# A four-network graph kernel: the nodes' update and the next products as one stage between two edge loops

## What is computed

```python
h = h @ W_in + b_in
def layer(hc, p):
    w1, b1, w2, b2, m1, c1, m2, c2 = p
    m = jnp.concatenate([hc[row], hc[col]], axis=1)
    m = jax.nn.silu(m @ w1 + b1)
    m = jax.nn.silu(m @ w2 + b2)
    agg = jax.ops.segment_sum(m, row, num_segments=N)
    z = jax.nn.silu(jnp.concatenate([hc, agg], axis=1) @ m1 + c1)
    return (hc + (z @ m2 + c2), None)
h, _ = jax.lax.scan(layer, h, (eW1, eb1, eW2, eb2, nW1, nb1, nW2, nb2))
return h @ W_out + b_out
```

## Time and profile before

| | |
|---|---|
| Median of three runs | 12523.31 us (12512.99 to 12532.43) |
| The profiled execution, its own time | 12525.73 us |
| Its span in the trace | 12523.9 us |
| Busy in the span: PE, DVE, ACT, POOL | 9274.0, 5811.6, 1419.6, 8101.0 us |
| Mean granted clock of PE | 0.764 of full |

### The profile page before, as it was taken

The page is one execution under the profiler, slowest core; times in us unless marked ns, Lnnn a source line. Parts: engine busy times, 40 slices in busy tenths (PEclk is TensorE's granted clock), DMA queues, the critical chain, the costliest instruction groups (busy, mean ns, idle before and its releaser), DMA issues. The chain is left out here.

```text
span 12523.9 us, 184074 instructions
## 1 busy us (share of the span) xinstructions
PE 9274.0 (74%) x46241; PEld 7382.7 (59%) x46242; DVE 5811.6 (46%) x14093; ACT 1419.6 (11%) x2535; POOL 8101.0 (65%) x8276
## 2 busy tenths in 40 slices
PE   3777888777677767776777899999993558785333
PEld 1665444566566656665666677777763547674333
DVE  9773000344344434443444455555557754443333
ACT  0002333111111111111111000000000001110000
POOL 3777777777477747774776577776760007775776
PEclk6557889677777777777777899999995658886555
DMA  1333443222222222222222687777772212221111
GB/s 56 102 109 124 142 136 129 65 52 52 40 65 52 52 54 52 52 52 42 52 52 41 169 205 204 205 204 204 203 190 60 87 44 64 64 63 30 26 26 26
DMA packets 818891, 1141.33 MB, mean 91 GB/s; under 512 B 245286, under 2 KB 442294, under 8 KB 817332
## 3 DMA queue, kind: packets, MB, share of 16 engines
q1 hardware_dynamic: 367186, 610.56, 17.7%
q0 software_dynamic: 277888, 340.47, 13.0%
q10 hardware_dynamic: 173666, 188.57, 4.6%
HBM read 939.74 MB, written 199.09 MB: 91 GB/s over the span
## 5 line engine op out<-in xcount | busy, mean ns | idle before, releaser
L1086 POOL DMA_INDIRECT gx_l<-xr,gi_l x4160 | 4007.4, 963 | 2579.8 <-DVE gi_l L1170 1314.5
L1575 PE MATMUL psum<-cw,xa 128*128 128x256 f32 (+1 forms) x8320 | 2116.0, 397 | 0.0
L1575 PEld LDWEIGHTS psum<-cw,xa 128*128 128x128 f32 (+1 forms) x8320 | 1442.6, 189 | 611.7 <-issue 482.4
L1192 DVE TENSOR_TENSOR aggT_l<-aggT_l,psum 64x128 f32 x4160 | 1158.6, 279 | 865.3 <-DVE aggT_l L1192 727.7
L1243 PE MATMUL psum<-ptab,oht 128*128 x6656 | 1176.6, 351 | 378.1 <-issue 204.5
L1243 PEld LDWEIGHTS psum<-ptab,oht 128*128 128x128 f32 x6656 | 1116.0, 262 | 477.4 <-issue 476.0
L1204 DVE TENSOR_TENSOR pre_s_l<-psum,gx_l 128x512 f32<-128x512 f32 x520 | 359.6, 691 | 1988.2 <-DMA gx_l<-xr,gi_l 1929.6
L1563 POOL DMA_INDIRECT wkv<-wtab,ei x832 | 908.5, 1092 | 453.4 <-issue 364.1
L706 POOL DMA_INDIRECT slots_s<-rec_s,row_s x806 | 812.2, 1008 | 399.9 <-issue 395.7
L1556 POOL DMA_INDIRECT gx<-xr,gi x832 | 788.4, 948 | 373.4 <-issue 252.9
L2133 POOL DMA_INDIRECT gx_l<-xr,gi_l x832 | 797.1, 958 | 332.8 <-issue 237.1
(11 more groups left out here) (341 smaller groups left out, 11934.1 us busy)
## 6 DMA issues: line engine op xcount, KB each, us to landing
shb<-shT SPq DMA_DIRECT2D x1872, 128.0 KB
kr<-keyrow_s SPq DMA_DIRECT2D x416, 256.0 KB
gx_l<-xr,gi_l POOLq DMA_INDIRECT x4992
wtab<-eo ACTq DMA_DIRECT2D x152, 512.0 KB, 4.0
vtab<-kv ACTq DMA_DIRECT2D x208, 256.0 KB, 2.4
v_in<-vtab SPq DMA_DIRECT2D x104, 512.0 KB, 3.3
hT<-noderow SPq DMA_DIRECT2D x101, 512.0 KB
kr<-keyrow_d SPq DMA_DIRECT2D x208, 128.0 KB
```

Of the source, the lines that this page charges most:

```text
L1086: pool.indirect_dma_start(gx[j][:, c_, :], None, xr, bass.IndirectOffsetOnAxis(ap=gi[j][:, c_:c_ + 1], axis=0)).then_inc(rows_in[j].sem, 16)
L1192: ins = dve.tensor_tensor(a, a, sums(j, h), ALU.add)
L1575: ins = pe.matmul(bank[2 + p][:, t % 2 * OKV:(t % 2 + 1) * OKV], xa[j][0:n_, c, t * P:(t + 1) * P], cw[0:n_, c, :], start=c == 0, stop=c = ...
```

## The change

The ten loads get three semaphores: product weights, edge weights, node weights. Layer 0's products are formed once ahead of the loop. Then each layer is an edge loop and one node stage. In that stage PE writes the first products alternately to banks 0, 1 and 2, 3, the second ones to banks 4 and 5, and the next layer's products (in the last layer the output's) to banks 6 and 7, straight from hT; its written order is first(0), first(1), second(0), first(2), second(1), products(0), first(3), and so on. z1T and qst have a second buffer each. The bias is split at the stage's start, aggT cleared at its end. Between layers one join is left, ahead of the edge loop. The chunks' column copies, turning and eviction stand at the start of the edge loop, where PE then waits until all is evicted; SP stores the features and loads the node weights, the next chunks and the next product weights inside the loop, behind its third key load. Behind the last layer the output stage is gone, and the layer norm stands ahead of the keys' copies.

```diff
+        qst_b = chunks.enter_context(nc.sbuf_tensor("qst_b", [P, CH, D], F32))
...
-        def edge_messages(o, local, feature=None):
+        def edge_messages(o, local, feature=None, opening={}):
...
                         sp.dma_start(kr[j][:], keyrow[o][bass.ds(i * (W * P), W * P)].partition_broadcast(P)).then_inc(keys_in[j].sem, 16)
+                        if k.fixed and k.t == 2 and "sp" in opening:
+                            opening["sp"]()
...
             join()
+            if "chunk" in opening:
+                opening["chunk"]()
...
-            join()
+            if feature:
+                join()
...
+        qsts = [qst, qst_b]
+        z1s = [z1T, hcur]
...
+        def product_weights_sp(l):
+            w1_in.at(sp.dma_start(w1[:], L0_eW1[l:l + 1, :, :].rearrange("a (k p) f -> p (a k) f", p=P)), 16)
+            w1_in.at(sp.dma_start(b1[:], L0_eb1[l:l + 1, :].rearrange("a f -> (a f)").partition_broadcast(P)), 16)
+            w1_in.at(sp.dma_start(b2r[:], L0_eb2[l:l + 1, :].rearrange("a f -> (a f)").partition_broadcast(3)), 16)
...
+        def edge_weights_sp(l):
+            for k in range(2):
+                w2_in.at(sp.dma_start(w2[k * D:(k + 1) * D, k * D:(k + 1) * D], L0_eW2[l:l + 1, :, :].rearrange("a p f -> p (a f)")), 16)
...
+        def node_weights_sp(l):
+            m_in.at(sp.dma_start(m1a[:], L0_nW1[l:l + 1, 0:HID, :].rearrange("a p f -> p (a f)")), 16)
...
+        def first_products():
+            product_weights_sp(0)
+            edge_weights_sp(0)
+            node_weights_sp(0)
+            dve.wait_ge(w1_in.sem, w1_in.n)
+            split_bias(b2r[:], b2[:], b2w)
+            pe.wait_ge(w1_in.sem, w1_in.n)
+            meet()
+            node_products(hcur, hT, w1)
+            scatters_end()
+            dve.memset(aggT[:], 0.0)
+            sp.wait_ge(w2_in.sem, w2_in.n)
+            sp.nop(nofuse=True)
...
         def layer(l):
-            wi = loaded
-            wi.at(sp.dma_start(w1[:], L0_eW1[l:l + 1, :, :].rearrange("a (k p) f -> p (a k) f", p=P)), 16)
...
-            wi.at(sp.dma_start(c2[:], L0_nb2[l:l + 1, :].rearrange("a (p f) -> p (a f)", f=1)), 16)
-            if l > 0:
...
+            last = l + 1 == LAYERS
+
+            def while_edges_sp():
...
+                if l:
+                    features_out_sp(l)
+                    node_weights_sp(l)
+                if not last:
+                    chunk_sp(l + 1)
+                    product_weights_sp(l + 1)
+
+            def chunk_first():
+                chunk_dve(l)
                 chunk_pe(l)
                 chunk_act(l)
-            dve.wait_ge(wi.sem, wi.n)
-            split_bias(b2r[:], b2[:], b2w)
-            meet()
-            node_products(hcur, hT, w1)
-            if l == 0:
-                scatters_end()
-            else:
-                chunk_dve(l)
-                features_out_sp(l)
-            step(dve.memset(aggT[:], 0.0))
-            if l + 1 < LAYERS:
-                chunk_sp(l + 1)
-            edge_messages("s", gather_p)
-            z_silu, z2_done, h_set = sig("z_silu"), sig("z2"), sig("h_set")
-
...
+            edge_messages("s", gather_p, opening={"sp": while_edges_sp, "chunk": chunk_first} if l else {"sp": while_edges_sp})
+            node_stage(l, last)
+
+        def node_stage(l, last):
+
+            added = sig("added")
+            z_silu, z2_done, h_set, formed, p_kept, summed_up = (sig(x) for x in ("z_silu", "z2", "h_set", "formed", "p_kept", "x_added"))
+            out_ps = bank[6][:, 0:CH * D].rearrange("p (b f) -> p b f", f=D)
+            next_ps = PS[:, 6 * 512:6 * 512 + CHN].rearrange("p (b k f) -> p b k f", b=CH, k=2)
+
+            def stage_pe():
+                pe.wait_ge(added.sem, added.n)
+                pe.wait_ge(m_in.sem, m_in.n)
+                pe.wait_ge(w1_in.sem, w1_in.n)
+                pe.nop(nofuse=True)
...
+                def first_of_two(i):
+                    if i >= 2:
...
-                        ins = pe.matmul(bank[k][:, 0:HALF], m1b[:], aggT[:, s_], start=False, stop=True)
+                        to = bank[2 * (i % 2) + k][:, 0:HALF]
+                        pe.matmul(to, m1a[:], hT[:, s_], start=True, stop=False)
+                        ins = pe.matmul(to, m1b[:], aggT[:, s_], start=False, stop=True)
...
+                def second_of_two(i):
                     pe.wait_ge(z_silu.sem, z_silu.n + i + 1)
                     if i:
                         pe.wait_ge(h_set.sem, h_set.n + i)
...
+                        ins = pe.matmul(bank[4 + k][:, 0:HALF], m2[:], z1s[i % 2][:, k * HALF:(k + 1) * HALF], start=True, stop=True)
                     ins.then_inc(z2_done.sem, 1)
...
-            def update_act():
+                def products(i):
+                    pe.wait_ge(h_set.sem, h_set.n + i + 1)
+                    if i and last:
+                        pe.wait_ge(summed_up.sem, summed_up.n + i)
+                    elif i:
+                        pe.wait_ge(p_kept.sem, p_kept.n + i)
+                        pe.wait_ge(evicted.sem, evicted.n + i)
...
+                    for b in range(CH):
+                        h_ = hT[:, i * CHN + b * P:i * CHN + (b + 1) * P]
...
+                            ins = pe.matmul(PS[:, 6 * 512 + b * P:6 * 512 + (b + 1) * P], h_, w1[:].rearrange("p k f -> p (k f)"), start=True, stop=True)
+                    ins.then_inc(formed.sem, 1)
+
+                first_of_two(0)
+                first_of_two(1)
                 for i in range(NCH):
+                    second_of_two(i)
+                    if i:
+                        products(i - 1)
+                    if i + 2 < NCH:
+                        first_of_two(i + 2)
+                products(NCH - 1)
+
...
+                def silu(i):
                     act.wait_ge(product.sem, product.n + i + 1)
-                    if i:
...
-                    act.activation(z1T[:].rearrange("p (k n) -> p k n", k=2), halves(0), ACT.Silu, bias=c1[:, 0:1]).then_inc(z_silu.sem, 1)
...
+                    if i >= 2:
+                        act.wait_ge(z2_done.sem, z2_done.n + i - 1)
...
+                    act.activation(z1s[i % 2][:].rearrange("p (k n) -> p k n", k=2), of, ACT.Silu, bias=c1[:, 0:1]).then_inc(z_silu.sem, 1)
...
+                def evict(i):
+                    act.wait_ge(p_kept.sem, p_kept.n + i + 1)
+                    if i >= 2:
+                        act.wait_ge(kept_in[i % 2].sem, kept_in[i % 2].n + 16 * (i // 2))
+                    act.copy(qsts[i % 2][:], next_ps[:, :, 1, :]).then_inc(evicted.sem, 1)
+
+                silu(0)
+                silu(1)
                 for i in range(NCH):
+                    if i and not last:
+                        evict(i - 1)
+                    if i + 2 < NCH:
+                        silu(i + 2)
+                if not last:
+                    evict(NCH - 1)
...
+                if not last:
+                    split_bias(b2r[:], b2[:], b2w)
...
+                    dve.scalar_tensor_tensor(s_, halves(4), c2[:, 0:1], s_, ALU.add, ALU.add).then_inc(h_set.sem, 1)
...
+                def keep(i):
+                    dve.wait_ge(formed.sem, formed.n + i + 1)
+                    dve.tensor_tensor(ptab[:, i * CH * D:(i + 1) * CH * D].rearrange("p (b f) -> p b f", f=D), next_ps[:, :, 0, :],
...
+                def add(i):
+                    dve.wait_ge(formed.sem, formed.n + i + 1)
+                    s_ = xn[:, i * CH:(i + 1) * CH, :]
+                    dve.tensor_tensor(s_, s_, out_ps, ALU.add).then_inc(summed_up.sem, 1)
+                    dve.wait_ge(summed_up.sem, summed_up.n + i + 1)
+                    step(dve.tensor_tensor(s_, s_, b_out[:].unsqueeze(1).broadcast_to([P, CH, D]), ALU.add))
...
+                for i in range(NCH):
+                    h(i)
+                    if i:
+                        add(i - 1) if last else keep(i - 1)
+                add(NCH - 1) if last else keep(NCH - 1)
+                if not last:
+                    step(dve.memset(aggT[:], 0.0))
...
+            def stage_sp():
+                sp.wait_ge(added.sem, added.n)
+                sp.nop(nofuse=True)
+                edge_weights_sp(l + 1)
+                for i in range(NCH):
+                    sp.wait_ge(evicted.sem, evicted.n + i + 1)
+                    sp.nop(nofuse=True)
+                    sp.dma_start(xr[i * CHN:(i + 1) * CHN, :].rearrange("(b p) f -> p b f", p=P), qsts[i % 2][:]).then_inc(kept_in[i % 2].sem, 16)
+                for j in range(2):
+                    sp.wait_ge(kept_in[j].sem, kept_in[j].n + 16 * len(range(j, NCH, 2)))
+                sp.wait_ge(w2_in.sem, w2_in.n)
+                sp.nop(nofuse=True)
+
+            stage_pe()
+            stage_act()
+            stage_dve()
+            if last:
+                summed_up.n += NCH
+                meet()
+            else:
...
                 x.n += NCH
-            meet()
...
+        first_products()
...
         keys_pe("d", done.n)
+        layernorm(xn)
```

(47 more changed lines are left out.)

48 lines of the change are left out of this document (14 added, 34 removed).

## The result

The changed kernel takes 12377.78 us (median of 4 runs, 12362.95 to 12384.67), the kernel before 12527.87 beside it (4 runs, 12512.99 to 12536.31): 0.988 of it, 95% interval 0.9863 to 0.9897, 150 us less where 167 were forecast. The profiled execution took 12384.67 us, span 12382.9; by medians it should be some 7 us less.

A forecast was written before the change was run, and what follows sets the result against it. POOL's gathers were taken to bound the edge loops, with time to win only where POOL stands still. Gaps between layers 151.9, behind the last layer 12.0 and ahead of layer 0 3.3 sum to 167.2 us: 12356 us, range 12330 to 12407.

The forecast's parts named there:

- What bounds the loops: Edge loops: POOL's 832 gathers set each loop's length, about 1050 us; what can be won lies where POOL stands still.
- The stage on PE, 33.9 us: Node stage on PE: 11.2 us at half clock, 14.8 and 6.75 at the high one, 1.1 waiting; together 33.9 us.
- The first rival: Node stage: PE waits in each group for sum, keep and eviction, 46.6 us against 33.9; total 12407 us; chance 0.11.
- The third: Node stage: clock stays low throughout, 21.6 us takes twice as long, four times; total 12442 us; chance 0.06.
- the fifth: Node stage: clock high from the start, first two groups' first products 5.6 us less, four times; 12334 us; chance 0.04.
- From its end to POOL, s + 39.7: Gaps between layers: first gather 39.7 us after the update's start s (stage 33.9, then clearing, copies); three layers win 151.9 us.
- Behind the last layer, 12.0 us: Gap behind the last layer, from the update's start s to POOL's next gather: 83.4 us against 95.37, 12.0 us won.
- Ahead of layer 0, 3.3 us: Before layer 0's loop: DVE waits for only three of ten loads, bias split done earlier; 3.3 us won.
- The opening costs nothing: Start of edge loops: chunk turning and feature stores beside gathers cost nothing; slack 12.6 us, about 26 in layer 3.
- The second rival: Feature stores in the edge loop drain at half speed beside gathers, 22.3 us more; total 12375 us; chance 0.09.
- The fourth: Edge loops: SP holds the fourth key load, POOL stands in turn 7; stores five times as long, 12572 us; chance 0.03.
- The sum: Whole kernel: 151.9 + 12.0 + 3.3 = 167.2 us won, median 12356 us, 1.3% less; chance 0.66.

## Why the prediction was right, and where not

*What bounds the loops*: right. No new wait of POOL inside a loop, and the gain is the gaps'.

*The stage on PE, 33.9 us*: 34.2 to 34.4. The slow clock lasted 13.7 to 15.6 us (from the means of 0.80 to 0.77), not 11.2, and the one wait was 1.24, not 1.1; that the sum is off by 0.3 us only has some luck in it. The first rival, a stage that stays serial, was wrong for this order and right for the other: as a kernel of its own it costs 70 us, not the 51 that I gave it, since its waits also bring the low clock. The third, the clock low throughout, was seen only with such waits, in one stage of four; the fifth, high at once, was seen only with PE busy to within 0.7 us of the stage's first product.

*From its end to POOL, s + 39.7*: s + 40.6 in layer 0 (3394.89 - 3354.31). Gains of the three gaps 150.3 us against 151.9.

*Behind the last layer, 12.0 us*: 11.7. The first gather was put at s + 83.4 and came at 6804.74 - 6721.34 = 83.4.

*Ahead of layer 0, 3.3 us*: 3.4.

*The opening costs nothing*: the step that was off, by 4 to 7 us (4.1 against the same trace's layer 0, 6.9 against the trace of before). The part about SP was right: stores in 23.2 us where I had 22.3, keys at 55.9 us behind the join where I had 54.3, the sum of turn 3 ended at 62 where I had 60.3, and no idle time in turn 7. The second rival, stores at half speed, is refuted by that same row; of the rule about queues taking turns the stores beside gathers show 0.9 us. The fourth needs more: it took twice the stores to make POOL stand for 14.39 and 12.35 us. What I left out is what comes behind a late turn: I wrote that DVE catches up since a turn costs it 6.0 us against POOL's 10.1, and counted only who waits. While it catches up, its comparisons meet the gathers at other places than in a steady turn, and more gathers are held, four of them through two comparisons; 9.0 us more gather time in the first twelve turns of three loops. POOL is the bound, so such time is lost without any wait of POOL.

*The sum*: 167.2 forecast, 158.5 found in the stretches that the change touches, 150 by medians. Of the miss 6.9 us are the loops (2.8 of them may be the run's), 1.9 the gaps, and the last 8 are within the 10 us to either side by which both kernels scatter.

## What to carry over

Where one engine's steady chain bounds the loops, the time is in the places where that chain stands; there it pays to move away whatever the next step of the chain does not need, and here that was worth more (89 us) than merging and pipelining the stages (56 us). Slack must be counted on each queue that the moved work passes, and the catching up behind it too: an engine that makes up for lost time can slow the bounding one without ever making it wait, so look at the longest of its instructions and not at their mean. A stage behind a stand of PE starts at half clock; dummy products kept it at the full one where they reached up to 0.7 us before that product, and not where they ended 2 us ahead.

## What I had not expected of the hardware

- An indirect DMA of 0.94 us on POOL took up to 2.62 us beside two DVE comparisons over 1024 columns, and ended 0.82 us behind the second, four times in the changed kernel. Of the other gathers that began under the first of the two 398 of 400 ended 0.82 us behind that one and took 1.0 to 1.5 us.
- 5.18 us of dense products followed by 2 us of standing did not keep the clock: the stage ran at half clock for its first 13.7 us, about as long as without them, and in one layer for 20.5 us after 1.5 us at the high one. With 0 to 0.7 us of standing it stayed at 1.00.
- The same program takes 12.5 ms on one chip and 16.8 to 17.0 on two others, where PE, ACT and DVE stand together in the loops.
